# Keys and values of the context in one block with all layers, context in halves, first cross attention's first parts made beside them, query groups spread over the lead-in

## The reference, cut to what matters

```python
# first layer: the context is normalised
yn = layernorm(y, ln2_w, ln2_b)
kv = (yn @ Wkv)                       # keys and values, 384 -> 2 x 512
# second layer: the raw context, keys with a bias
k = kv_in @ wk.T + bk
v = kv_in @ wv.T + bv
# cross attention of both, x normalised first
q = (xn @ Wq); attn = softmax(q k^T * scale); x = x + (attn v) @ Wproj + bproj
```

## Time and profile before

| | |
|---|---|
| median of 3 runs | 3268.69 us (3267.51 to 3273.05) |
| the profiled execution's own time | 3269.26 us |
| its span, first to last instruction | 3267.4 us |
| PE (tensor engine, matmul) busy | 3135.3 us, 96% of the span |
| DVE busy | 1818.6 us, 56% |
| ACT busy | 1574.4 us, 48% |
| POOL busy | 1314.2 us, 40% |
| mean granted clock of the tensor engine | 0.984 |

### The profile page before, as it was taken

The page is one execution under the profiler, slowest core; times in us unless marked ns, Lnnn a source line. Parts: engine busy times, 40 slices in busy tenths (PEclk is TensorE's granted clock), DMA queues, the critical chain, the costliest instruction groups (busy, mean ns, idle before and its releaser), DMA issues.

```text
span 3267.4 us, 41887 instructions
## 1 busy us (share of the span) xinstructions
PE 3135.3 (96%) x14480; PEld 2496.2 (76%) x14480; DVE 1818.6 (56%) x2854; ACT 1574.4 (48%) x2984; POOL 1314.2 (40%) x1357
## 2 busy tenths in 40 slices
PE   6699999999999998999999999979999999999999
PEld 5478877888888876677777777657887888888887
DVE  4588884323223235887888788868888432222221
ACT  3366663322222234767776777756666322222222
POOL 0344551333332325666666666745455111111110
PEclk9799999999999999999999999989999999999999
DMA  4323223211111123344344334432222311111110
GB/s 147 112 68 90 84 75 123 74 52 52 46 42 40 49 103 101 101 127 119 102 120 124 107 108 118 122 89 77 82 83 79 120 52 39 39 39 39 39 39 13
DMA packets 215045, 264.33 MB, mean 81 GB/s; under 512 B 78459, under 2 KB 100579, under 8 KB 214835
## 3 DMA queue, kind: packets, MB, share of 16 engines
q1 hardware_dynamic: 214323, 260.87, 27.0%
q10 hardware_dynamic: 512, 0.79, 0.1%
HBM read 125.12 MB, written 60.42 MB: 57 GB/s over the span
## 4 chain that ended last, share of the span: by engine, by line
PE 83%; DVE 6%; issue 2%; SPq 2%; ACT 2%; DMA 1%; POOL 1%; ACTq 0%; DVEq 0%; POOLq 0%
PE L1sa_o L1085 5%; PE L1ff_f L110 4%; PE L1ff_f L112 4%; PE L1ff_f L111 4%; PE L1ff_acc L112 4%; PE L0ff_acc L110 4%; PE L1ff_acc L110 4%; PE L1ff_acc L111 4%; PE L0ff_f L110 4%; PE L0ff_acc L112 4%; PE L0ff_acc L111 4%; PE L0ff_f L112 4%; PE L0ff_f L111 4%; PE L1sa_pj L110 3%; PE L1sa_s L1040 3%; PE L1sa_pj L111 3%
## 5 line engine op out<-in xcount | busy, mean ns | idle before, releaser
L1221 DVE TENSOR_REDUCE L1sa_nmax<-L1sa_s 128x2 f32<-128x1024 f32 x256 | 310.3, 1212 | 121.9 <-PE L1sa_s L1040 121.3
L350 DVE TENSOR_TENSOR L1ff_gl<-L1ff_gf,L1ff_gh 128x512 fp32r<-128x512 f32 x128 | 95.4, 745 | 469.4 <-ACT L1ff_gh L336 469.4
L1313 POOL TENSOR_TENSOR L1sa_El<-L1sa_E,L1sa_Eh 128x1024 fp32r<-128x1024 f32 x122 | 299.7, 2457 | 119.6 <-ACT L1sa_Eh L1140 119.6
L350 DVE TENSOR_TENSOR L0ff_gl<-L0ff_gf,L0ff_gh 128x512 fp32r<-128x512 f32 x128 | 96.3, 752 | 415.0 <-ACT L0ff_gh L336 415.0
L324 ACT ACTIVATE L1ff_gf<-L1ff_f,cols 128x512 f32<-128x512 f32 x128 | 88.3, 690 | 452.6 <-PE L1ff_f L112 452.6
L324 ACT ACTIVATE L0ff_gf<-L0ff_f,cols 128x512 f32<-128x512 f32 x128 | 88.3, 690 | 431.4 <-PE L0ff_f L112 431.4
L1147 ACT ACTIVATE L1sa_E<-L1sa_st 128x1024 f32<-128x1024 f32 x256 | 258.7, 1011 | 5.4 <-PE L1sa_st L1052 5.3
L110 PE MATMUL L0ff_acc<-L0ff_Wh,L0ff_gh 128*128 128x512 f32 x512 | 200.3, 391 | 6.8 <-DVE L0ff_gl L350 6.8
L1140 ACT ACTIVATE L1sa_Eh<-L1sa_E 128x1024 fp32r<-128x1024 f32 x196 | 204.8, 1045 | 0.1
L110 PE MATMUL L0ff_f<-L0ca_hTh,L0ff_Wh 128*128 128x512 f32 x512 | 202.5, 396 | 0.0
L110 PE MATMUL L1ff_f<-L0ca_hTh,L1ff_Wh 128*128 128x512 f32 x512 | 202.1, 395 | 0.0
(11 more groups left out here) (310 smaller groups left out, 8495.7 us busy)
## 6 DMA issues: line engine op xcount, KB each, us to landing
L1sa_OLN<-L1sa_osb SPq DMA_DIRECT2D x127, 192.0 KB, 2.7
L1sa_stack_q<-L1sa_parts_q SPq DMA_DIRECT2D x128, 128.0 KB, 2.6
L1sa_stack_k<-L1sa_parts_k SPq DMA_DIRECT2D x124, 128.0 KB, 2.6
L0ff_xs<-x SPq DMA_DIRECT2D x60, 256.0 KB, 3.0
L1ff_xs<-x SPq DMA_DIRECT2D x60, 256.0 KB, 3.5
L0ca_stage<-in_x SPq DMA_DIRECT2D x32, 256.0 KB, 2.8
x<-L0ca_stage SPq DMA_DIRECT2D x32, 256.0 KB, 2.1
L0ff_stage<-in_L_w SPq DMA_DIRECT2D x32, 256.0 KB, 3.2
```

Of the source, the lines that this page charges most:

```text
L350: nc.vector.tensor_tensor(gl[:, j % 2, :], gf[:, j % 2, :], f32(gh[:, j % 2, :]), ALU.subtract)\
L1221: nc.vector.reduce_max(nmax[:, h % 2, 2 * (n % 2):2 * (n % 2) + 2], s_bank[:, :, :], AX.X, negate=True)\
L1313: nc.gpsimd.tensor_tensor(El[:, n % 2, :], E[:, n % 3, :], f32(Eh[:, n % 2, :]), ALU.subtract)\
```

## The change

The diff touches only the program's beginning. It has six parts.

1. `context_kv` is no longer a block and a phase with semaphores and a barrier of its own: its engine programs stand in the same block as the layers, ahead of L0ca's. Its buffers lie at fixed addresses (`KV_SPOTS`) beside those that L0ca needs early; its semaphores are used again by L0ff and L1sa, counting on from where they ended.
2. The context is loaded in two halves of 4 batches, and the T units of index 0 take the first half's units first.
3. Three store buffers for keys and three for values in place of two.
4. The T units of index 1 stand between the V units of index 0, and their split is another: ACT makes `tmp`, DVE copies it to the high part and makes the low part.
5. L0ca's beginning stands beside units of `context_kv`: loads of batch 0 behind stores of keys of index 0, query weights behind stores of values of index 0, zeros on POOL, statistics and normalisation on DVE behind the K units of index 1, its four transposes as X units between the V units of index 1, the split of the query weights behind V units 2 and 4, the keys of batch 0 behind the store of V unit 3, the loads of batch 1 behind that of V unit 5. The values of batch 0 are placed when all stores have landed.
6. For L0ca the lead-in starts when one query group is made; groups 1, 2 and 3 are made ahead of tiles 2 and 4 and behind tile 5. L1ca stays as it was.

The diff, cut to its core:

```diff
     def events(self, name, per=1, unit=1, skip=0, batches=None):
-        if self.earlier is None:
+        if self.earlier is None and self.spent:
+            before = self.spent.pop()
+            self.counts[name] = Count(before.sem, per, unit, skip, batches, before.end)
+        elif self.earlier is None:
...
+def context_kv(nc, ph, block, cst, ctx_in, layers):
+    RING = 3
...
+    units = [("T", 0, i) for i in (0, 2, 4, 1, 3, 5)] + [("K", 0, i) for i in range(8)]
+    for i in range(B):
+        units += [("T", 1, j) for j in range(6) if j == i - 1] + [("V", 0, i)]
+    units += [("K", 1, i) for i in range(8)]
+    for i in range(B):
+        units += [("V", 1, i)] + [("X", 1, c) for c in range(KT) if c == i - XV]
...
-            sp.dma_start(x[:, :, :], ctx_in.rearrange("b l d -> l b d")).then_inc(e_x.sem, e_x.unit)
+            for i in range(2):
+                half = slice(i * B // 2, (i + 1) * B // 2)
+                sp.dma_start(x[:, half, :], ctx_in[half].rearrange("b l d -> l b d")).then_inc(e_x[i].sem, e_x[i].unit)
...
+                if (kind, layer) == ("K", 0) and i >= 4:
+                    ca.first_load(sp, i - 4)
+                if (kind, layer) == ("V", 0) and i in (1, 3):
+                    ca.first_weights(sp, i // 2)
+                if (kind, layer, i) == ("V", 1, KEYS_AT):
+                    all_stored(sp, "K", 8 * NL)
+                    ca.first_keys(sp)
+                if (kind, layer, i) == ("V", 1, 5):
+                    ca.second_loads(sp)
+            all_stored(sp, "V", B * NL)
...
+                if kind == "X":
+                    ca.T(pe, 0, i, banks[place[u] % 8])
+                    continue
...
+            ca.first_products(pe)
+            evacuated(pe, own[-1])
...
+                if kind == "X":
+                    ca.whole(act, 0, i)
+                    continue
...
+                    nc.scalar.activation(tmp[:, i % 2, :], bank_of((kind, layer, i)), ACT.Identity, bias=ln_b[:, c:c + 1],
+                                         scale=ln_w[:, c:c + 1]).then_inc(e_hf.sem, e_hf.unit)
...
+                    nc.vector.tensor_copy(hi, tmp[:, i % 2, :]).then_inc(e_th.sem, e_th.unit)
...
+                if (kind, layer) == ("K", 1):
+                    if i < TT:
+                        ca.statistics(dve, i)
+                    else:
+                        ca.normalise(dve, 0, i - TT)
+                if (kind, layer) == ("V", 1) and i in WQ_AT:
+                    ca.weights_lo(dve, WQ_AT.index(i))
+            ca.first_low(dve)
...
+            pool.wait_ge(wt.lo.sem, wt.lo.no(2 * NL - 1))
+            for i in range(2):
+                ca.zeros(pool, i)
+            pool.wait_ge(e_unit.sem, e_unit.no(no["V", 0, B - 1]))
+            for i in range(2, 4):
+                ca.zeros(pool, i)
+            ca.rsqrt(pool, 0)
+            for c in range(KT):
+                ca.lo(pool, 0, c)
...
+WQ_AT, KEYS_AT, XV = (2, 4), 3, 0
...
+    if sa is None:
+        FIRST, MADE, SPLIT = 1, {2: (1,), 4: (2,), LEAD: (3,)}, {1: (1,), 3: (2,), LEAD - 1: (3,)}
+    else:
+        FIRST, MADE, SPLIT = 2, {2: (2, 3)}, {1: (2,), LEAD - 1: (3,)}
...
-            for s in range(LEAD):
-                if s == 2:
-                    for kind, b, i in CA_FIRST[2:]:
-                        for c in range(KT):
-                            piece(pe, kind, b, i, c)
+            for s in range(LEAD + 1):
+                for i in MADE.get(s, ()):
+                    for c in range(KT):
+                        piece(pe, *CA_FIRST[i], c)
```

268 lines of the change are left out of this document (131 added, 137 removed), and 4 rows, old and new, of the table KV_SPOTS.

## The result

The changed kernel takes 3226.06 us (median of 4 runs, 3221.53 to 3226.97), the one before beside it 3268.72; the ratio is 0.9864, with a 95% interval of 0.9847 to 0.9881. A second set gave 3224.29 us and 0.9865 (0.9850 to 0.9880). The forecast was 3223 and a range of 3217 to 3233. The profiled execution took 3221.53 us, 47.7 us less than the profiled one before; the medians lie 43 to 45 us apart. The profiled execution is the quickest of its four, the other three took 3225.5 to 3227.0, so its trace shows a win that is 3 to 5 us above the usual one.

A forecast was written before the change was run, and what follows sets the result against it. PE, busy 96% of the span, was taken as the bound except at the beginning; 48.0 us won at L0ca's first maximum, less 1.0 and 1, gave 46 and about 3223 us, eight times in ten 3217 to 3233.

The forecast's parts named there:

- Start: First products near 14.8 us through the halved context load: 1.8 us won, or 1.0 if the halves end later.
- Values 0: First V units of index 0 start at 28.0 us, after the weights' low part; PE waits 0.6 us instead of 2.4.
- T units between values, keys 1: Values of index 0 with T units end at 47.1 us; keys of index 1 take 10.1, to 57.2.
- Values 1 with X units: V units of index 1 with four X units: 16.8 us plus 1.9 for transposes, to 75.9 us.
- Mark: Start of L0ca's first maximum at 80.8 us, 48.0 earlier than 128.81; band 79 to 84.
- Lead-in: Stretch behind L0ca's first maximum: between 3.5 us lost and 3 won through later query groups; 1 us lost taken.
- Clock stays high: Rival: in the lead-in 3 us are won instead of 1 lost; 3213 to 3219 us; chance 0.10.
- Stores set the pace: Rival: stores land later beside the new loads and cost units 7 to 20 us; 3230 to 3243; chance 0.13.
- Clock stays low: Rival: products up to the first maximum run at half clock; 3250 us if half of them do; chance 0.02.
- Slower: Rival: stores land so late behind new loads that units take 3.6 us or more; chance 0.01.
- The change does not do what it says: Halves land together and group 0 alone starts no earlier: costs 1.8 + 2.8 us, 3227, inside the forecast's range.
- Sum: Whole kernel: 48.0 less 1.0 for the lead-in, less 1 for later landings, gives 46 us won.

The follow-up runs named there:

- e0: The changed kernel run once more without any edit: 3224.3 us, ratio 0.9865 to the kernel before.
- e4: Changed kernel with the six T units of index 1 behind all V units of index 0 again, not between them: 3230.8 us, ratio 0.9876.
- e6: Changed kernel with each X unit one value unit later, behind value units 1 to 4: 3224.0 us, ratio 0.9860.
- e7: Changed kernel with the normalisation of batch 1's tokens on DVE ahead of the fifth maximum, not the third: 3228.6 us, ratio 0.9872.
- e2: Changed kernel with the context loaded in one transfer again instead of two halves: 3226.3 us, ratio 0.9864.
- after: The changed kernel itself, first set and first trace: 3226.1 us, ratio 0.9864 to the kernel before.
- e3: Changed kernel with query groups as before, two ahead of the first score tile and two ahead of the third: 3223.3 us, ratio 0.9856.
- e8: Changed kernel with the low part of the values' weights ahead of key unit 3's low part on DVE: 3220.9 us, ratio 0.9853.
- e1_loads_late: Changed kernel with L0ca's beginning, loads included, behind the context's list on every engine: 3246.5 us, ratio 0.9925.

## Why the prediction was right, point by point

**Bounds now.** Right. What was won at the mark stayed won: 45.9 us there, 47.9 to 48.1 at every maximum from the twenty-fifth on, 47.7 at the end of the profiled pair.

**Start.** 1.44 us won in place of 1.8; 0.9 to 2.5 over the twelve traces with halves.

**Values 0.** The step "28.0" held in the first trace (28.34), and its order (store, unit 3's low part, weights' low part) was the right one. Its size is not a number but a spread: 28.1 to 30.9 in the seven other traces with three buffers and this order (e0 to e4, e6, e7; the 30.9 is e2's, which starts 2 us late, the next is 30.3). The prediction gave it one value from one trace of before, and its terms, 24.6 + 0.52 + 0.54 + 0.4 + 1.75, make 27.8.

**T units between values, keys 1.** Right to 0.3 us: 19.0 and 10.16 us against 19.1 and 10.1.

**Values 1 with X units.** This is the term that missed: the products took the 18.6 us that were forecast, but PE waited 1.6 for the tokens. The prediction called DVE's work under the keys tight and priced it at nothing; a late key store (ACT waited 3.0 us for one at 54.8) and the root on POOL came on top. The wait was 0.8 to 2.8 us in the six traces with this order and three buffers (after, e0, e2, e3, e7, e8).

**Mark.** 82.87 and 85.06 against 80.8; the band of 79 to 84 held for one of two. Two more of the prediction's own signs failed: it allowed PE no wait above 1.5 us, and there is one of 1.6 in the first trace and one of 3.5 in the second, the latter behind a store, which it had named as a sign of being wrong.

**Lead-in.** The 1 us lost, as a sum, is 0.8 by the fifth maximum, and for the reasons given (group 2's split ahead of it). By the thirteenth it was won back in the first trace, by the clock; in e0, where the clock fell, the lead-in is 0.9 us longer than before. The prediction had weighed the two against each other and set the sum at 1 lost.

**The rivals.** *Clock stays high* was half right and so wrong: the clock did stay at 1.00 in the first trace's lead-in, where before it had fallen to 0.51 for 12 us, and group 3's high part still came 14.1 us behind the mark, 0.9 later than before (0.8 was forecast for 12 products at 0.23 ahead of it). Idle time that is left there belongs to other engines' order. The clock is worth something all the same: in e0, where it fell, this high part came 1.6 us later, and from the fifth to the thirteenth maximum it takes 17.6 us in the first trace, 19.2 in e0 and 19.1 before. That is 1.6 of the up to 3 us that the prediction named. Of the 2.5 us in the first keys nothing came back: PE is busy 13.0 us with them, 12.5 before. *Stores set the pace* did not happen, though the new loads lengthened some landings from about 3 us to 5; two buffers show how near it was. *Clock stays low* and *Slower* did not happen: the windows up to the mark are at 1.00 in the first trace, and the lowest in e0 is 0.91, over values 0. *The change does not do what it says*: the halves land apart, at the start, and are not seen at the end.

**Sum.** 46 us was forecast and 47.7 came in the profiled pair, 43 to 45 in the medians. The mark gave 45.9 where 48.0 was forecast. Behind it came 0.7 in the lead-in instead of a loss of 1, and 1.2 to 1.4 of clock that nothing in the change explains; both cover the wait of 1.6 and the later start, and the 1 us taken off for landings beside the new loads (3.3 MB by the issues, not 4) fell due at a store that these loads don't touch. So the total is better than its parts, and that it came within 3 us is in part luck.

## What to carry to other kernels

Ask what stands behind an operation that waits for a store, and give such a step a spread, not a value: here a weight's low part, needed by all that follows, stood behind one on DVE, and moving it up gave the lowest ratio of all small edits, though within the intervals. Work that is hidden beside a bound engine must also be ready when that engine comes to it: X units without their tokens cost 1.6 us, and T units moved one place further cost 4.5. Removing a boundary between stages gave 4 of 46 us, the new order inside the context's list 20, and loading and preparing the next stage beside the products of the last one 22, so that is where to look first. Read a kernel's clock by stretches before crediting an edit with 1 or 2 us.

## What the runs showed of the hardware

- Three stores of 308 KB, issued within 0.05 us of the same times in two executions of one kernel, moved their data at the same rates (219 and 216 GB/s from 22.0 to 26.3 us), and yet let ACT have the first buffer at 25.05 us in the one and at 27.03 in the other.
- Key stores among loads of tokens landed 5.2 and 5.1 us after their issue, the same ones without these loads 2.7 and 3.3 (e1_loads_late).
- The profile's granted clock reads 1.00 from 15.09 us on, and yet products of 308 columns stand 0.26 us apart until 21.2 us and 0.14 from there. At 178.5 us before the change, 0.26 is their spacing at a granted clock of 0.52. So at the start of these traces the spacing of the products tells PE's pace, and that column does not.
- PE at the lower of its two clock levels turned up in single stretches of a few microseconds in one execution and not in the next of the same kernel: a mean of 0.66 from 95 to 100 us in e0, after 3.3 us of work in 5, and 1.00 at that place in the other trace, after 3.1 in 5. Products of 512 columns then stand 0.43 us apart instead of 0.23. Between these two executions the mark differs by 2.2 us and the lead-in by 1.6, and the whole time by 2.6. Whether landings and clock explain the 5 us between the quickest and the slowest of one set is not shown, as only one execution of each run has a trace.
